# Moving the six squares of the LayerNorm statistics from VectorE to GpSimd, and holding GpSimd's opening transfers back until the first chunk of x has landed

## The reference

```python
xn = layernorm(x)                       # over the 1024 channels, eps 1e-5
k = xn @ Wk.T ; r = xn @ Wr.T           # 1024 x 1024 each
# WKV recurrence along the tokens, v = r; per channel
y = wkv_scan(-exp(time_decay), time_first, k, r)
attn = (sigmoid(r) * y) @ Wo.T
gate = xn @ (w_gate/127).T ; up = xn @ (w_up/127).T      # HIDDEN 3072
ffn = (silu(gate) * up) @ (w_down/127).T
out = x + attn + ffn
```

## Time and profile before

| | |
|---|---|
| median of 3 runs | 1967.3 us (1966.03 to 1967.64) |
| the profiled execution's own time | 1966.2 us |
| its span, slowest core (core 3) | 1964.3 us; 1.9 us lie around the span |
| spans of the 8 cores | 1957.1 to 1964.3 us |
| DVE busy | 797.0 us (41%) |
| PE busy | 1467.8 us (75%) |
| POOL busy | 31.0 us in 43 instructions, memsets and DMA issues |
| phase A | to about 851 us, chunks about 99 us each |

### The profile page before, as it was taken

One profiled execution on the slowest core, in us unless ns is written; L12 is line 12 of the kernel. 1 busy time (PEld: TensorE's weight loads), 2 busy tenths in 40 slices (PEclk: granted clock), 3 DMA queues, 4 the chain that ended last, 5 costly groups with the idle time before them and its releaser, 6 DMA issues.

```text
span 1964.3 us, 17671 instructions; the slowest of 8 cores (1957.1 to 1964.3 us)
## 1 busy us (share of the span) xinstructions
PE 1467.8 (75%) x6368; PEld 629.2 (32%) x6368; DVE 797.0 (41%) x1331; ACT 363.4 (18%) x621; POOL 31.0 (2%) x43
## 2 busy tenths in 40 slices
PE   1537474747474646512999999999999999999997
PEld 0213131313121212201444444444444444444443
DVE  2687878787878786800111112111111111111111
ACT  0232323232323232300110101101011011010110
POOL 0000000000000000000000000000000000000000
PEclk9678787878787877765999999999999999999998
DMA  9900909090909010178002002020020020300201
GB/s 193 150 0 1 171 0 171 1 167 5 162 10 157 15 64 1 65 232 259 1 22 86 1 22 86 1 98 10 22 86 1 23 85 0 107 1 22 86 1 43
DMA packets 47108, 129.05 MB, mean 66 GB/s; under 512 B 1392, under 2 KB 9584, under 8 KB 46448
## 3 DMA queue, kind: packets, MB, share of 16 engines
q0 software_dynamic: 14512, 67.11, 17.0%
q1 hardware_dynamic: 32512, 60.83, 9.9%
HBM read 111.16 MB, written 60.82 MB: 88 GB/s over the span
## 4 chain that ended last, share of the span: by engine, by line
PE 51%; SPq 2%; DMA 1%; DVE 1%; issue 0%; DVEq 0%; POOL 0%; POOLq 0%
PE psB_gu L639 17%; PE psB_gu L650 17%; PE psB_d L684 9%; PE psB_d L666 8%; DMA xnb<-xn_scr 1%; DVE pb L599 1%; SPq L560 1%; SPq L568 0%; SPq L556 0%; PE psB_d L673 0%; SPq L564 0%; DVE pb L606 0%; POOL out_cm L695 0%; DVEq L543 0%; SPq L552 0%
## 5 line engine op out<-in xcount | busy, mean ns | idle before, releaser
L592 DVE SCALAR_TENSOR_TENSOR h_act<-psB_gu,silu 128x512 bf16<-128x512 f32 x192 | 132.7, 691 | 751.3 <-PE psB_gu L650 751.3
L639 PE MATMUL psB_gu<-xnb,wgbf 128*128 128x512 bf16 x1536 | 364.5, 380 | 79.3 <-DMA xnb<-xn_scr 79.3
L650 PE MATMUL psB_gu<-xnb,wubf 128*128 128x512 bf16 x1536 | 363.4, 379 | 0.0
L621 ACT ACTIVATE silu<-psB_gu 128x512 f32<-128x512 f32 x192 | 114.6, 597 | 885.1 <-PE psB_gu L639 885.1
L639 PEld LDWEIGHTS psB_gu<-xnb,wgbf 128*128 128x128 bf16 x1536 | 150.5, 98 | 261.7 <-issue 81.4
L650 PEld LDWEIGHTS psB_gu<-xnb,wubf 128*128 128x128 bf16 x1536 | 150.5, 98 | 181.9 <-issue 1.3
L684 PE MATMUL psB_d<-h_act,wdbf 128*128 128x512 bf16 x768 | 177.2, 395 | 22.8 <-DVE pb L599 22.8
L666 PE MATMUL psB_d<-h_act,wdbf 128*128 128x512 bf16 x736 | 188.9, 379 | 0.0
L422 PE MATMUL ps_wo<-outpre,wo_bf 128*128 128x512 bf16 x448 | 115.3, 416 | 92.2 <-DVE xn_buf L376 77.9
L438 PE MATMUL ps_k<-xn_buf,wk_bf 128*128 128x512 bf16 x512 | 134.3, 410 | 37.2 <-ACT k_sb L175 26.2
L447 PE MATMUL ps_r<-xn_buf,wr_bf 128*128 128x512 bf16 x512 | 122.8, 383 | 0.0
(11 more groups left out here) (117 smaller groups left out, 906.7 us busy)
## 6 DMA issues: line engine op xcount, KB each, us to landing
x_buf<-x_cm SPq DMA_DIRECT2D x8, 2048.0 KB, 38.2
pt_scr<-x_buf POOLq DMA_DIRECT2D x8, 2048.0 KB, 11.7
pb<-pt_scr SPq DMA_DIRECT2D x8, 2048.0 KB, 9.0
out_cm<-pb POOLq DMA_DIRECT2D x8, 2048.0 KB, 8.3
xn_scr<-xn_buf POOLq DMA_DIRECT2D x8, 1024.0 KB, 44.4
xnb<-xn_scr SPq DMA_DIRECT2D x8, 1024.0 KB, 5.3
wg_bfd<-wgT POOLq DMA_DIRECT2D x4, 1536.0 KB, 61.8
wu_bfd<-wuT POOLq DMA_DIRECT2D x4, 1536.0 KB, 32.7
```

The source lines that it names most:

```text
L592: ve.scalar_tensor_tensor(out=h_act[:, hg * TC:(hg + 1) * TC], in0=up_sl(hg), scalar=1.0 / 127.0, in1=silu[hg % 2], op0=Alu.mult, op1=Alu. ...
L621: sc.activation(out=silu[hg % 2], in_=gate_sl(hg), func=Act.Silu, scale=1.0 / 127.0).then_inc(sem["s_sil"], 1)
L639: ins = te.matmul(gate_sl(hg), wgbf[:, gc * HID + hg * D:gc * HID + (hg + 1) * D], gsl(xnb, gc), start=(gc == 0), stop=(gc == G - 1))
L650: ins = te.matmul(up_sl(hg), wubf[:, gc * HID + hg * D:gc * HID + (hg + 1) * D], gsl(xnb, gc), start=(gc == 0), stop=(gc == G - 1))
```

## The change

Two edits. The first takes the squares of chunks 2 to 7 from VectorE's program (L378 to L382, six instructions of 128x4096) and puts them into GpSimd's, between its DMA issue of xn_scr for chunk j and its wait for v_res of chunk j. There GpSimd waits for the landing of x chunk j+2, for the landing of chunk j's store to xn_scr, and for t_rog = 8j+8 (TensorE has finished reading the xn_buf that is overwritten). The squares of chunks 0 and 1 stay on VectorE. The second edit makes GpSimd wait for the landing of x chunk 0 ahead of its first DMA, the load of Wk, and so ahead of all the DMAs that it issues behind it.

```diff
@@ VectorE, at the end of chunk j
-                    if j + 2 < NCH:
-                        ve.wait_ge(*sa_x(j + 2))
-                        ve.wait_ge(*g_xn_done(j))
-                        ve.tensor_mul(xn_buf[(j + 2) % 2], x_buf[(j + 2) % 3],
-                                      x_buf[(j + 2) % 3]).then_inc(sem["v_sq"], 1)
+
@@ GpSimd
             def _(gp):
+                gp.wait_ge(sem["sA_x0"], 16)
                 gp.dma_start(
                     out=wk_bf.rearrange("p (g n) -> p g n", n=1024),
...
                         in_=xn_buf[j % 2].rearrange("p (g t) -> p g t", t=TC),
                     ).then_inc(sem[f"g_xn{j % 2}"], 16)
+                    if j + 2 < NCH:
+                        gp.wait_ge(*sa_x(j + 2))
+                        gp.wait_ge(*g_xn_done(j))
+                        gp.wait_ge(sem["t_rog"], 8 * j + 8)
+                        gp.tensor_mul(xn_buf[(j + 2) % 2], x_buf[(j + 2) % 3],
+                                      x_buf[(j + 2) % 3]).then_inc(sem["v_sq"], 1)
                     gp.wait_ge(sem["v_res"], 8 * j + 8)
```

## The result

| | before | after |
|---|---|---|
| median of 8 runs each | 1967.74 us | 1984.42 us (1982.43 to 1985.71) |
| ratio of after to before, 95% interval | | 1.0085 [1.0074, 1.0097] |
| profiled execution, slowest core's span | 1964.3 us (core 3) | 1984.1 us (core 7) |
| spans of the 8 cores | 1957.1 to 1964.3 us | 1974.7 to 1984.1 us |

Two of the 8 runs before (2207.62 and 2132.28 us) were slow ones, and every ratio here leaves such runs out. The change makes the kernel 0.85% slower, 16.7 us. The forecast was 36.8 us slower (2003.0 against 1966.2). The sign and the mechanism are those of rival A; the size is less than half.

What follows compares the result with a forecast made beforehand. Bound taken: in phase A, DVE itself to the last subtraction, then PE, ScalarE and the first scan group, with phase B untouched. 1966.2 + 45.8 (DVE held up) - 9 (opening) = 2003.0 us, range 1956 to 2014.

Steps and rivals of the forecast that it cites:

- rival A: Normalisation and scan groups: two-input DVE instructions stand while GpSimd's square reads, 45.8 us lost, total 2003 us; chance 0.5.
- Part 1, L381 leaves for nothing: Chunk boundary: six squares, 26.5 us of VectorE busy time, leave without gain because PE and ScalarE waits hide them.
- Part 2, when the square starts: Chunks 1 to 5: GpSimd's square starts when x lands, about 246.1 us for chunk 1; chunk 0's near 101.
- Part 2, the duration: One GpSimd square of 128x4096: estimated 8.8 us, between 4.42 and 13.3, costing nothing by itself.
- Part 2, the collision: DVE's two-input instructions held by the square: 7.4 us in each of chunks 1 to 5, 8.8 in chunk 0, 45.8 total.
- Rival B: DVE and GpSimd interleave, DVE stretched to 1.5 times while both read: 22.9 us lost, total 1980 us; chance 0.2.
- Rival C: No loss on DVE from the squares, only the opening counts: total 1957 us (1954 to 1962); chance 0.2.
- Part 3, the opening: Start of the kernel: x chunks land earlier, Wr becomes the last wait for the first projection; gain 9 us, low end 4.
- Rival D: The opening gives nothing, Wr landing as late as v_xn did or later: 2012 or 1966 us; chance 0.1.
- The sum: Whole kernel: 1966.2 us profiled, plus 45.8 for the collision, minus 9 for the opening, gives 2003.0 us.

Runs made afterwards that it cites:

- experiment 1: Kernel before plus only GpSimd's wait for x chunk 0 ahead of the Wk load, squares on VectorE: 1958.89 us, ratio 0.9947.
- experiment 3: Changed kernel, with each GpSimd square of chunk j+2 also waiting for the end of chunk j+1's normalisation: 1956.55 us, ratio 0.9938.
- experiment 2: Changed kernel without the opening wait, so only the move of the six squares is kept: 2003.18 us, ratio 1.0171.
- experiment 4: Changed kernel, with GpSimd filling xn_buf with ones in place of the squares, writing without reading: 1959.06 us, ratio 0.9953.
- experiment 5: Changed kernel, with each GpSimd square issued as eight 128x512 instructions in place of one of 128x4096: 1978.53 us, ratio 1.0057.
- experiment 6: Changed kernel, with each GpSimd square made twice, the second an instruction of its own behind the first: 2021.27 us, ratio 1.0264.
- experiment 8: Kernel of experiment 1, with the load of x chunk 2 also waiting until Wr has landed: 1949.51 us, ratio 0.9909.

## Why the prediction was right or wrong

**Part 1, L381 leaves for nothing: right.** In the changed kernel DVE's waits behind the last subtraction grew by what left. At the start of chunk 2 on core 7 the two residual additions wait 4.03 and 1.46 us for TensorE (0 and 1.07 in the earlier trace rows), the scan group still 4.76 us for ScalarE. Experiments 1 and 3 settle it: with the squares on DVE or, harmlessly placed, on GpSimd, the time is the same (1958.89 and 1956.55 us, with intervals that overlap), and the cores lose the same 0.6 us in the mean behind the opening.

**Part 2, when the square starts: 1.4 us too late.** I took 246.1 on core 3, 1.4 us before L372 and 3.2 us after the last row maximum, for all five chunks and all cores. The trace before could have said otherwise: over its 8 cores the x loads land 0.8 to 4.0 us after the last row maximum, 2.4 in the mean. In the changed kernel the squares of chunks 1 to 5 start 1.8 us after it in the mean (from 1.2 us before it to 4.8 after); on core 7 of the changed kernel the five fall between the last row maximum and L365. The x loads land 36.6 us after issue there and not 38.1. A square that starts while DVE still has its one-input row maxima, or just ahead of the 3.15 us in which DVE waits for msb_sb, is partly free: chunks 2 and 3 on core 7 lose 4.3 and 2.8 us.

**Part 2, the duration: the term that was mis-sized most.** I estimated 8.8 us, with 4.4 and 13.3 as ends. It is 7.0 us wherever nothing held it up. For six squares that is 10.8 us of the sum. With 7.0 in my own formula, 7.0 + 5 x (246.1 + 7.0 - 247.5), the sum is 35.0 us; experiment 2, with the opening of before, lost 35.0 us over the cores and 33.6 in time. So the formula held where its start times did, with some luck: there the squares start 3.4 us after the last row maximum in the mean, and chunk 0 lost 6.0 us and not 7.0. The Trainium skill (GPSIMD Engine Reference, section 3.1) would have given 9.0 us, as an estimate; its figure is for an addition of float32 elements, and the measurement decides here.

**Part 2, the collision (rival A): right.** DVE stands until the square ends. Experiments 3, 4, 5 and 6 tell it from the others: the block of two-input instructions needs GpSimd's reading (4) and both inputs in SBUF (3), lasts one instruction (5), and grows with its length (6). L361, which mere writing blocks as well (4), was in no part of the forecast. Rival B, a stretch to 1.5 times, would have given multiplications of 1.0 us: none is seen except where pieces alternate. Rival C is out for this placement, and its number is just what experiment 3 makes of it. The Trainium skill (SBUF — State Buffer, section "Who interferes with whom") had said that a VectorE instruction with two SBUF inputs is blocked by a GpSimd instruction that reads SBUF, and the trace agrees: 0.75 us become 7.30.

**Part 3, the opening: right in size, by luck in part.** 9 us were forecast; 9.9 us is the mean of the cores in experiment 1 and 10.4 us the gain in time. Wr was the last wait, as worked out. But two steps were wrong and nearly cancel. x chunk 0 landed at 16.4 us in the mean of the cores and not at 11, so Wr was issued 6 us later than I took, at 18.1 us. And Wr landed 41.3 us after its issue where I had kept the 51.3 of before, so it landed at 59.4 us, against the 59.9 to 63.3 that I gave. A load alone from phase B was too good a row for x chunk 0; with only chunk 1 issued beside it (experiment 8) it still lands at 16.1 us, and a load alone at the start was not tried. Chunk 1 came 8.5 us behind chunk 0 and not 20. Rival D is out.

**The sum.** Forecast +45.8 - 9 = 36.8 us. The step that failed is the size of the collision term: 45.8 us were forecast and 30.4 are measured in the mean of the cores. The duration, 7.0 and not 8.8 us, took 10.8 of it (45.8 to 35.0). The other 4.6 are 3.1 in chunks 1 to 5 (24.9 against 28.0), where the squares start earlier, 0.8 in chunk 0, and 0.7 that chunk 6 gives back. The duration alone would leave 26 us, so it is not the whole of the miss. With 10.7 us for the opening, 1.7 more than forecast, 19.7 remain on the mean core. The two profiled executions differ by 19.4 us (1985.6 and 1966.2) and the medians by 16.7; the rest is the spread between executions. The two edits do not add up because the starts moved earlier once the opening wait is there: the squares start 1.8 us after the last row maximum in the changed kernel and 3.4 in experiment 2 (means of the cores), and chunks 1 to 5 lose 24.9 and 29.6 us. Of these 1.6 us, 1.2 are the x loads, which land 36.5 us after their issue and not 37.7. What makes them sooner was not tried.

## What to carry to other kernels

Moving an instruction off a busy engine gains nothing where the engine waits behind it anyhow; look at what ends the next wait, not at the busy share. Arithmetic on GpSimd that reads SBUF costs VectorE up to its own length where VectorE has two-input SBUF instructions on the path, so place it by a wait into a stretch where VectorE has none (waits, reductions, instructions with a PSUM input), or leave it where it was. Look at the small one-input instructions of that stretch too: L361 was held here, even by a fill. In an opening, order the transfers by who waits first, and look again at what has become last: here a wait ahead of the weights moved the bound to Wr, and holding back one more load moved it on.

## What the runs showed of the hardware that was not expected

GpSimd's square of 128x4096, float32 in and bfloat16 out, both inputs the same tile, took 7.00 us wherever VectorE did not hold it up, and up to 8.0 us where it did (7.98 on core 6 of the changed kernel); in pieces of 128x512 it took 1.03 us each, 8.2 us in all. Even a 128x8 instruction of VectorE waits for the whole square: on core 7 of the changed kernel L365 was held for 6.97 us in chunk 2. L361, with one input, was held by a fill that reads nothing (3.27 us in place of 0.17 on core 7 of experiment 4). And the casting loads of the weights are slower with the x loads beside them: Wk landed 30.9 us after its issue and 17.4 us in experiment 8, and Wr landed 12.9 us behind Wk there (17.5 + 17.4 against 18.55 + 29.3), where it had been 21.4.
